# Two attention blocks on one core: later key blocks' scores from differences of keys, in pairs of tiles

## The chip, the cores and the metric

One core of one Trainium2 chip runs the kernel. The metric is device time in microseconds of one execution; the input arrays lie in device memory, laid out by the host, and the result is written back there. The granted clock of TensorE was full (1.00) in every stretch of the profile of the kernel before.

## The reference

Input x is 4 images of 64 channels with 32 x 32 positions, float32. Two layers follow each other, each for every image by itself:

```
h = group_norm(x, 32 groups) * gamma + beta
q, k, v = h Wq + bq, h Wk + bk, h Wv + bv         # 1024 positions, 64 channels
attn = softmax(q k^T / 8) v                       # 1024 x 1024 scores
x = x + attn Wo + bo
```

The two layers differ in their parameters and in the small constant under the root.

## The kernel before

A **unit** is one layer of one image; there are 8, and unit u+4 takes the result of unit u. An image lies in 128 partitions: the 64 channels of positions 0 to 511 in the upper half (rows 0 to 63), those of 512 to 1023 in the lower. So every product with 64 channels takes half the rows of TensorE's array, and two such products, one in each half of the rows, can go together.

Queries and keys are computed by `project` (L789) into `ps_scores[0]`. ScalarE (`high_front`, `high_back`, L380 to L389) writes them rounded to f32r, TensorE's fast number type, and VectorE (`low_front`, `low_back`, L570 to L582) what the rounding lost. `front` holds queries in its upper rows and keys in its lower rows, `back` the other way round, and `cross` gets the halves exchanged by four DMAs of 128 KB. The column halves are named HI and LO: the rounded part and the rest. The three buffers of each form a ring.

Softmax needs the greatest score of each query. `partial_max` (L808) computes rounded scores of 128 queries against 512 keys, twice, into the one buffer `ps_max`, 8 rounds per unit; after each, `part` (L584) on VectorE reduces 1024 columns. `join` brings the results together, `turn_max` (L829) transposes them, `stage_max` (L425) copies them, and `place_rows` (L229) writes them by DMA as a row `q_row`. The rounds for unit w+1 are spread over the loop of unit w, and the first two of unit w+2 follow in the same loop (`next_max(8)` and `next_max(9)`).

Scores come per tile of 128 keys against all 1024 queries, 8 tiles in a unit, in two alternating buffers `ps_scores` (in the last unit three). `scores_main` (L837) issues six half-array products of 512 columns: rounded by rounded, rounded keys by rest, rest by rounded queries. `scores_row` (L862) adds the negative maxima by two more products, `ones_r` by `q_row`. `exp` (L431) on ScalarE writes `probs[t]`; `values` (L874) on TensorE adds the tile's part of the result to `ps_attn`, and GpSimd (`add`, L306) sums the eight tiles, after `first_add` (L614) on VectorE. From the sum `denominators` (L904) makes column sums in 256 columns, two `reciprocal`s (L621) of 128 columns each invert them, eight DMAs spread them over the partitions as `rden`, and `finish` (L315) on GpSimd scales the result and adds x.

The order on every engine is written out by hand; each engine runs its list in order and stops at a wait on a semaphore. In the loop of TensorE (L1053) two or three steps of scores, maxima and values alternate; the projection for unit w+2 stands in the middle, after scores(w, 5).

Of the kernel before, what the change touches and what calls it, by code (L numbers as in the profile page):

```python
# [5 lines left out]
ALU = mybir.AluOpType  # L6
# [5 lines left out]
P = 128  # L12
# [18 lines left out]
def attention_pair(nc, x, layer_params, consts, out):  # L31
# [6 lines left out]


    B, _, HALF = x.shape  # L40
    N = 2 * HALF
    TILES = N // P
    UNITS = LAYERS * B
    LAST = UNITS - 1
    SCALE = float(C) ** -0.5
    JS = HALF // P
    POOL_ADDS = TILES - 2
    TAIL_ADDS = (4, 1)
    HEAD_MAX = [0, 1, 2, JS, JS + 1, JS + 2, 3, JS + 3]
    READY = 3 * P  # L50

    with ExitStack() as ctx:
# [13 lines left out]
        back_w = [sb(f"back_w{n}", [P, P]) for n in range(LAYERS)]  # L66
        back_bias = [sb(f"back_bias{n}", [P, 1]) for n in range(LAYERS)]
        const_sb = sb("const_sb", [P, 2 * P])
        ident = const_sb[:, 0:P]
        ones = sb("ones", [P, 2 * P])  # L70
        ones_r = sb("ones_r", [P, P], F32R)
        minus_half = sb("minus_half", [P, 1])
# [12 lines left out]
        front = [sb(f"front{b}", [P, N], F32R) for b in range(RING)]  # L85
        back = [sb(f"back{b}", [P, N], F32R) for b in range(RING)]
        cross = [sb(f"cross{b}", [P, N], F32R) for b in range(RING)]
        full_front = sb("full_front", [P, HALF])
        full_back = sb("full_back", [P, HALF])
        q_row = [sb(f"q_row{b}", [P, HALF], F32R) for b in range(2)]  # L90
# [3 lines left out]
        max_cols = sb("max_cols", [P, TILES * C])  # L94
# [5 lines left out]
        pick = sb("pick", [P, 4 * C])  # L100
        quarter_rden = sb("quarter_rden", [P, HALF // 2])
# [4 lines left out]
        ps_attn = psum("ps_attn", [P, HALF])  # L106
        ps_misc = psum("ps_misc", [P, HALF])
# [5 lines left out]
        ones_r_set = sem("ones_r_set")  # L113
        half_set = sem("half_set")
# [3 lines left out]
        cols_zero = sem("cols_zero")  # L118
        pick_zero = sem("pick_zero")
        pick_set = sem("pick_set")  # L120
        back_set = sem("back_set")
# [10 lines left out]
        front_hi = sem("front_hi")  # L132
        back_hi = sem("back_hi")
        front_full = sem("front_full")
        back_full = sem("back_full")
        front_lo = sem("front_lo")
        back_lo = sem("back_lo")
        first_back_hi = sem("first_back_hi")
        head_front_lo = sem("head_front_lo")
        head_back_lo = sem("head_back_lo")  # L140
# [9 lines left out]
        head_turned = sem("head_turned")  # L150
# [13 lines left out]
        quarter_done = sem("quarter_done")  # L164
# [11 lines left out]

        def halves():
            return (slice(0, HALF), slice(HALF, N))
# [13 lines left out]
        HI, LO = slice(0, HALF), slice(HALF, N)  # L192

        def back_hi_of(unit):
            return (back_hi, unit) if unit else (first_back_hi, 1)
# [7 lines left out]
        def scores_buffer(unit, t):  # L203
            return ps_scores[t % 2] if unit < LAST else (ps_scores[0], ps_scores[1], ps_max)[t % 3]
# [4 lines left out]
        def _(sp):  # L209
# [5 lines left out]
            def swap_hi(u):  # L215
                t = cross[u % RING]
                sp.wait_ge(front_hi, u + 1)
                sp.dma_start(t[0:C, HI].bitcast(F32), front[u % RING][C:P, HI].bitcast(F32)).then_inc(hi_swapped[u % RING], 16)
                sp.wait_ge(*back_hi_of(u))
                sp.dma_start(t[C:P, HI].bitcast(F32), back[u % RING][0:C, HI].bitcast(F32)).then_inc(hi_swapped[u % RING], 16)  # L220

            def swap_lo(u):
                t = cross[u % RING]
                sp.wait_ge(*low_count(front_lo, head_front_lo, u))
# [4 lines left out]
            def place_rows(u):  # L229
                sp.wait_ge(max_staged, u + 1)  # L230
                if u == 1:
                    sp.wait_ge(rows_zero, 1)
# [32 lines left out]
            for w in range(UNITS):  # L265
                if w:
                    spread_rden(w - 1)
                if w + 2 < UNITS:
                    swap_hi(w + 2)
                    swap_lo(w + 2)  # L270
# [915 lines left out]
```

## Time and profile before

| | |
|---|---|
| median of 3 runs | 185.75 us (185.75 to 185.83) |
| span of the profiled execution | 184.0 us (its total time is not on the page) |
| instructions | 3303 |
| TensorE busy | 174.6 us, 95% |
| VectorE busy | 138.3 us, 75% |
| GpSimd busy | 121.8 us, 66% |
| ScalarE busy | 100.4 us, 55% |

The span goes from the first to the last instruction. Engines are named PE (TensorE; PEld its weight loads), DVE (VectorE), ACT (ScalarE), POOL (GpSimd) and SP. Waiting is not busy time. The rows print f32r products as f32; the lines tell them apart. An f32 product appears as two instructions, its two passes.

### The profile page before, as it was taken

The page shows a single profiled execution, that of the slowest core. Times are in us where ns is not written, and L with a number is a line of the kernel's source. Part 1 is how long each engine was busy: PE and PEld are TensorE (multiplying, and loading weights), DVE is VectorE, ACT ScalarE, POOL GpSimd, SP SyncE. Part 2 cuts the span into 40 slices and gives each one's busy share as a digit, 9 for nine tenths or more (in the row PEclk, how much of TensorE's full clock was granted, in tenths as well). Part 3 has the DMA queues.
Part 4 walks back from the last instruction along what each step waited for, and adds up shares of the span by engine and source line. Part 5 has one row for each costly group of instructions (what it writes and reads, how often), then busy time and mean ns, then how long its engine had stood idle before and what let it go on. Part 6 is the DMA issues. An engine that isn't in the chain of part 4 may idle for free.

```text
span 184.0 us, 3303 instructions
## 1 busy us (share of the span) xinstructions
PE 174.6 (95%) x1223; PEld 93.5 (51%) x1223; DVE 138.3 (75%) x208; ACT 100.4 (55%) x137; POOL 121.8 (66%) x81
## 2 busy tenths in 40 slices
PE   7778899999999999999999999999999999999993
PEld 4435545555525644455535645555535555456661
DVE  2799987779887687859875787769875588386763
ACT  3479367606656376436666476527656554466500
POOL 5265017996799929996699949996799939705000
PEclk9999999999999999999999999999999999999999
DMA  5544100500016000420025000500025100110111
GB/s 154 189 100 98 34 2 0 114 4 2 0 34 142 2 0 14 102 60 0 0 54 122 0 4 20 136 18 0 5 59 115 61 0 21 37 61 7 50 57 57
DMA packets 7103, 8.89 MB, mean 48 GB/s; under 512 B 1656, under 2 KB 4144, under 8 KB 7088
## 3 DMA queue, kind: packets, MB, share of 16 engines
q1 hardware_dynamic: 6080, 7.84, 16.9%
q10 hardware_dynamic: 1008, 0.86, 1.6%
q8 instruction: 9, 0.15, 0.3%
q14 instruction: 6, 0.05, 0.1%
HBM read 1.58 MB, written 1.05 MB: 14 GB/s over the span
## 4 chain that ended last, share of the span: by engine, by line
PE 82%; DVE 13%; DMA 1%; issue 1%; POOL 0%; ACT 0%; DVEq 0%; POOLq 0%
PE ps_attn L887 27%; PE ps_max L817 9%; DVE part_max L588 8%; PE ps_scores L855 8%; PE ps_scores L871 7%; PE ps_scores L857 7%; PE ps_scores L859 7%; PE ps_scores L796 3%; PE ps_misc L804 2%; PE ps_attn L894 2%; PE ps_misc L900 2%; DMA xs<-x_dram 1%; PE ps_misc L894 1%; DVE quarter_rden L628 1%; PE ps_misc L831 1%
## 5 line engine op out<-in xcount | busy, mean ns | idle before, releaser
L313 POOL TENSOR_TENSOR prob_sum<-prob_sum,probs 128x1024 f32<-128x1024 f32 x41 | 97.5, 2377 | 29.0 <-ACT probs L441 16.8
L588 DVE TENSOR_REDUCE part_max<-ps_max 128x2 f32<-128x1024 f32 x60 | 73.4, 1224 | 26.3 <-PE ps_max L818 25.8
L441 ACT ACTIVATE probs<-ps_scores 128x1024 f32<-128x1024 f32 x62 | 61.0, 1025 | 46.1 <-PE ps_scores L872 45.4
L887 PE MATMUL ps_attn<-probs,vals 128*64 128x512 f32 x224 | 54.5, 605 | 0.0
L887 PEld LDWEIGHTS ps_attn<-probs,vals 128*64 128x64 f32 x224 | 13.5, 136 | 27.8 <-issue 19.2
L871 PE MATMUL ps_scores<-q_row,ones_r 64*128 64x512 f32 x62 | 24.5, 396 | 0.5 <-ACT q_row L423 0.5
L872 PE MATMUL ps_scores<-q_row,ones_r 64*128 64x512 f32 x62 | 24.6, 396 | 0.0
L817 PE MATMUL ps_max<-back,front 64*128 64x512 f32 x31 | 13.9, 449 | 2.3 <-DVE part_max L588 1.4
L817 PE MATMUL ps_max<-cross,front 64*128 64x512 f32 x29 | 14.6, 505 | 0.3 <-DVE part_max L588 0.3
L818 PE MATMUL ps_max<-cross,back 64*128 64x512 f32 x29 | 14.6, 505 | 0.0
L818 PE MATMUL ps_max<-front,back 64*128 64x512 f32 x31 | 14.0, 450 | 0.0
L628 DVE RECIPROCAL quarter_rden<-ps_misc 128x128 f32<-128x128 f32 x14 | 12.6, 930 | 1.1 <-PE ps_misc L900 1.1
L871 PEld LDWEIGHTS ps_scores<-q_row,ones_r 64*128 64x128 f32 x62 | 11.4, 184 | 3.2 <-issue 0.7
L856 PE MATMUL ps_scores<-back,cross 64*128 64x512 f32 x31 | 12.9, 418 | 0.0
L294 POOL TENSOR_TENSOR rstd<-var_eps,minus_half 128x1 f32<-128x1 f32 x8 | 4.4, 549 | 12.9 <-DVE var_eps L543 12.9
L855 PE MATMUL ps_scores<-front,back 64*128 64x512 f32 x31 | 12.9, 415 | 0.0
L855 PE MATMUL ps_scores<-front,cross 64*128 64x512 f32 x31 | 12.4, 399 | 0.0
L856 PE MATMUL ps_scores<-back,front 64*128 64x512 f32 x31 | 12.4, 399 | 0.0
L860 PE MATMUL ps_scores<-back,cross 64*128 64x512 f32 x31 | 12.1, 392 | 0.0
L859 PE MATMUL ps_scores<-front,back 64*128 64x512 f32 x31 | 12.1, 391 | 0.0
L860 PE MATMUL ps_scores<-back,front 64*128 64x512 f32 x31 | 12.1, 390 | 0.0
L859 PE MATMUL ps_scores<-front,cross 64*128 64x512 f32 x31 | 12.1, 390 | 0.0
(157 smaller groups left out, 365.7 us busy)
## 6 DMA issues: line engine op xcount, KB each, us to landing
cross<-front SPq DMA_DIRECT2D x16, 128.0 KB, 2.3
cross<-back SPq DMA_DIRECT2D x16, 128.0 KB, 2.3
rden<-quarter_rden SPq DMA_DIRECT2D x44, 32.0 KB, 1.8
xs<-x_dram SPq DMA_DIRECT2D x4, 256.0 KB, 4.6
out_dram<-xs SPq DMA_DIRECT2D x3, 256.0 KB, 2.0
rden<-quarter_rden ACTq DMA_DIRECT2D x12, 32.0 KB, 1.9
q_row<-max_rows SPq DMA_DIRECT2D x14, 2.0 KB
layer<-layers_dram SPq DMA_DIRECT2D x1, 194.5 KB, 2.7
```

The source lines that it names most:

```text
L313: pool.tensor_tensor(total[:, :], total[:, :], probs[t][:, :], ALU.add).then_inc(added, 1)
L441: act.activation(probs[t][:, :], scores_buffer(u, t)[:, :], ACT.Exp, scale=SCALE).then_inc(exp_done, 1)
L588: dve.tensor_reduce(part_max[u % 2][:, at:at + 2 * JS + 1:2 * JS], ps[:, :].rearrange("p (g n) -> p g n", g=2), AX.X, ALU.max, negate=True ...
L817: pe.matmul(ps[:, HI], f[top, tile], (x if crossed else g)[top, HI], start=True, stop=True)
L818: pe.matmul(ps[:, LO], g[low, tile], (x if crossed else f)[low, HI], start=True, stop=True).then_inc(max_mm, 1)
L855: pe.matmul(left, key_top[top, hi], front_u[top, HI], start=True, stop=False)
L856: pe.matmul(right, key_low[low, hi], back_u[low, HI], start=True, stop=False)
L859: pe.matmul(left, key_top[top, lo], front_u[top, HI], start=False, stop=False)
L860: pe.matmul(right, key_low[low, lo], back_u[low, HI], start=False, stop=False)
L871: pe.matmul(left, ones_r[top, :], row[top, :], start=False, stop=True)
L872: pe.matmul(right, ones_r[low, :], row[low, :], start=False, stop=True).then_inc(scores_mm, 1)
L887: mm = pe.matmul(ps_attn[half * C:(half + 1) * C, :], v, probs[t][:, cols], start=(t == 0), stop=(t == TILES - 1))
```

## The change

1. **Tiles in pairs.** Tile t now stands for key block `(t % 2, JS - 1 - t // 2)`: the two tiles of a pair are the same block in the two halves of the keys, and both score buffers fill together. The first pair's scores are computed in full. For pairs 1 to 3 the products with *differences* between neighbouring key blocks are added to the scores that still stand in the buffers. A pair waits for both exponentials of the pair before it, not for one of two tiles before.
2. **Row products once per unit.** As the negative maxima stay in the buffers, `add_rows` adds them once, after the first pair, by 4 products in place of 16. `q_row` is 1024 columns wide. In unit 0 `add_maxima` does it by 16 products of 128 columns against the identity; `turn_first` and `stage_first` go.
3. **Queries exchanged.** `q_hi`, `q_lo` hold queries in all 128 rows, `x_hi`, `x_lo` the same with the halves exchanged (four DMAs as before); the keys `k_hi`, `k_lo` are followed by their three differences, 384 columns. `project` makes four products of 64 x 64, and from unit 2 on writes `ps_max` instead of `ps_scores[0]`. ScalarE does high_queries, whole_keys, high_keys, high_differences; VectorE low_queries, key_differences, low_keys.
4. **Maxima.** No maximum of unit w+2 runs in the loop of unit w any more; project(w+2) is the last but one step of the loop.
5. **Denominators in 128 columns.** Eight products of 128 columns with a 0/1 pattern `parity` in place of four of 256, one reciprocal in place of two, eight DMAs of 64 x 128.
6. In the last unit the scores no longer use `ps_max` as a third buffer.

The core of the diff:

```diff
             def project(u):
-                p = layer[u // B]
+                p, ps = layer[u // B], ps_scores[0] if u < HEAD else ps_max
                 pe.wait_ge(h_ready, u + 1)
...
+                elif u >= HEAD:
+                    pe.wait_ge(max_done, TILES * u)
+                wq, wk = slice(WQ, WQ + C), slice(WK, WK + C)
+                pe.matmul(ps[TOP, HI], p[TOP, wq], h[TOP, :], start=True, stop=True)
+                pe.matmul(ps[LOW, HI], p[LOW, wq], h[LOW, :], start=True, stop=True)
+                pe.matmul(ps[LOW, LO], p[TOP, wk], h[TOP, :], start=True, stop=True)
+                pe.matmul(ps[TOP, LO], p[LOW, wk], h[LOW, :], start=True, stop=True).then_inc(proj_mm, 1)
...
             def partial_max(u, m, ps=ps_max):
...
+                if u:
+                    pe.wait_ge(max_done, TILES * u + m - (m == 0 and u == 1))
                 if m == 0:
-                    pe.wait_ge(front_hi, u + 1)
-                    pe.wait_ge(*back_hi_of(u))
+                    pe.wait_ge(q_hi_set, u + 1)
+                    pe.wait_ge(*k_hi_of(u))
+                    if u >= HEAD:
+                        pe.wait_ge(k_full_set, u + 1)
+                        pe.wait_ge(q_lo_set, u + 1 - HEAD)
...
+            def product(u, p, keys, at, in_place, exchanged, start, done):
+                block = slice(at, at + P)
+                top, low = ps_scores[1], ps_scores[0]
...
+            def pair_high(u, p):
+                b = u % RING
+                at = DIFF + p * P if p == 0 else HALF + (JS - 1 - p) * P
+                product(u, p, k_hi[b], at, q_hi[b], x_hi[b], p == 0, False)
+                product(u, p, k_hi[b], at, q_lo[b], x_lo[b], False, False)
+
+            def pair_low(u, p):
...
+                mm = product(u, p, k_lo[b], at, q_hi[b], x_hi[b], False, True)
...
+            def pair(u, p):
+                pe.wait_ge(exp_done, TILES * u + 2 * p)
+                pair_high(u, p)
+                pair_low(u, p)
```

`product` issues four half-array products of 512 columns: keys of the upper rows into the two banks of `ps_scores[1]`, those of the lower rows into `ps_scores[0]`. The loop of TensorE for units 1 to 6 is now, in this order (w the unit, the maxima those of w+1):

```
first_pair(w)  max 0  pair_low(w, 0)  add_rows(w)  max 1  values(w-1, 6) values(w-1, 7)  max 2
pair(w, 1)  max 3  denominators(w-1)  values(w, 0) values(w, 1)  max 4  pair(w, 2)  max 5
values(w, 2) values(w, 3)  max 6  pair(w, 3)  max 7  values(w, 4) values(w, 5)  turn_max(w+1)
project(w+2)  project_v(w+2)
```

ScalarE's loop ends with exp(w, 6), exp(w, 7), stage_max(w+1), high_queries(w+2), whole_keys, high_keys, copy_v, high_differences. VectorE's is part 0, part 1, low_keys(w+1), own_stats(w+2), part 2, share_stats, join_stats, first_add(w), part 3, affine, part 4, reciprocal(w-1), parts 5 to 7, join(w+1), low_queries(w+2), key_differences.

TensorE at the end of a unit, before, from the transposition of unit 3's maxima on:

```order
L831 MATMUL ps_misc<-const_sb,neg_max 8x128 [waits max_joined,quarter_done]
L817 MATMUL ps_max<-back,front 128x512 [waits back_hi,front_hi,max_done]
L818 MATMUL ps_max<-front,back 128x512
L855 MATMUL ps_scores<-front,back 128x512 [waits exp_done,back_lo,front_lo]
L856 MATMUL ps_scores<-back,cross 128x512
L857 MATMUL ps_scores<-front,back 128x512
```

and in the changed kernel, from the same transposition:

```order
L809 MATMUL ps_both<-const_sb,neg_max 8x128 [waits rden_done,max_joined]
L774 MATMUL ps_max<-h,layer 64x512 [waits max_done,h_ready]
L775 MATMUL ps_max<-h,layer 64x512
L776 MATMUL ps_max<-h,layer 64x512
L777 MATMUL ps_max<-h,layer 64x512
L783 MATMUL ps_both<-wvo,h 64x128 [waits max_staged]
L783 MATMUL ps_both<-wvo,h 64x128 x7
```

Before, a maximum of the next unit and scores follow the transposition; now the projection into ps_max and that of the values do.

TensorE in the changed kernel a little later, from the last products of the projection of values to the first maximum of the next unit:

```order
L783 MATMUL ps_both<-wvo,h 64x128 x7
L814 MATMUL ps_scores<-q_hi,k_hi 128x512 [waits exp_done,k_lo_set,lo_swapped0]
L816 MATMUL ps_scores<-q_hi,k_hi 128x512
L818 MATMUL ps_scores<-x_hi,k_hi 128x512
L820 MATMUL ps_scores<-x_hi,k_hi 128x512
L814 MATMUL ps_scores<-q_lo,k_hi 128x512
L816 MATMUL ps_scores<-q_lo,k_hi 128x512
L818 MATMUL ps_scores<-x_lo,k_hi 128x512
L820 MATMUL ps_scores<-x_lo,k_hi 128x512
L802 MATMUL ps_max<-k_hi,q_hi 128x512 [waits k_full_set,k_hi_set,q_lo_set,q_hi_set,max_done]
L803 MATMUL ps_max<-k_hi,q_hi 128x512
```

The first maximum waits for five semaphores of ScalarE and VectorE; 8 score products stand ahead of it and 8 products behind it before the next maximum.

VectorE at the same boundary, before (neg_max is join's result, the lines after it make front's and back's rest):

```order
L611 TENSOR_REDUCE neg_max<-part_max 128x8 [waits max_turned,max_done]
L572 SCALAR_TENSOR_TENSOR front<-ps_scores,layer,front 128x512 [waits front_hi]
L579 SCALAR_TENSOR_TENSOR back<-ps_scores,back_bias,back 128x512 [waits back_hi]
L588 TENSOR_REDUCE part_max<-ps_max 128x2 [waits max_mm] x2
L522 BN_STATS stats<-xs 128x6 [waits final_done]
L588 TENSOR_REDUCE part_max<-ps_max 128x2 [waits max_mm]
```

and in the changed kernel:

```order
L623 TENSOR_REDUCE neg_max<-part_max 128x8 [waits max_turned,max_done]
L590 SCALAR_TENSOR_TENSOR q_lo<-ps_max,bias_q,q_hi 128x512 [waits q_hi_set]
L597 TENSOR_TENSOR k_full<-k_full 128x384 [waits k_full_set]
L609 TENSOR_REDUCE part_max<-ps_max 128x2 [waits max_mm] x2
L602 TENSOR_TENSOR k_lo<-k_full,k_hi 128x512 [waits d_hi_set,k_hi_set]
L541 BN_STATS stats<-xs 128x6 [waits final_done]
L609 TENSOR_REDUCE part_max<-ps_max 128x2 [waits max_mm]
```

low_front and low_back, which both stood ahead of the next rounds, became low_queries and key_differences there, and low_keys after the second round; `BN_STATS` moved behind it.

## Rows read from the trace of the kernel before

**Rows 1.** The page, busy us of each engine, share of the span, instructions.
```profile
PE 174.6 (95%) x1223; PEld 93.5 (51%) x1223; DVE 138.3 (75%) x208; ACT 100.4 (55%) x137; POOL 121.8 (66%) x81
```

**Rows 2.** Busy us in a steady stretch, by engine: stretch, busy (instructions).
```profile
96.50:117.00 20.50, 20.50 (x143) 10.68 (x141) 15.93 (x25) 11.85 (x15) 17.25 (x10) 1.00 0.18 41
```

**Rows 3.** The page, chain that ended last, share of the span by engine.
```profile
PE 82%; DVE 13%; DMA 1%; issue 1%; POOL 0%; ACT 0%; DVEq 0%; POOLq 0%
```

**Rows 4.** The page, groups of instructions: shapes, count, busy us, mean ns, idle before.
```profile
L588 DVE TENSOR_REDUCE part_max<-ps_max 128x2 f32<-128x1024 f32 x60 | 73.4, 1224 | 26.3 <-PE ps_max L818 25.8
L628 DVE RECIPROCAL quarter_rden<-ps_misc 128x128 f32<-128x128 f32 x14 | 12.6, 930 | 1.1 <-PE ps_misc L900 1.1
```

**Rows 5.** Waits: who waited for whom, us in total, times, longest.
```profile
PEld ps_max L817 <- DVE part_max L588: 13.9, 24, 1.2
```

**Rows 6.** Timeline of TensorE, one unit: start us, us, engine, line, operation, tiles, shapes.
```profile
96.95 0.50 PE L817 MATMUL ps_max<-back,front 64*128 64x512 f32 x1
97.29 0.39 PE L855 MATMUL ps_scores<-front,back 64*128 64x512 f32 x1
97.52 0.39 PE L857 MATMUL ps_scores<-front,back 64*128 64x512 f32 x1
...
104.73 1.94 PE L887 MATMUL ps_attn<-probs,vals 128*64 128x512 f32 x8
106.60 0.50 PE L817 MATMUL ps_max<-cross,front 64*128 64x512 f32 x1
...
117.23 0.27 PE L831 MATMUL ps_misc<-const_sb,neg_max 128*8 128x128 f32 x1
117.43 0.50 PE L817 MATMUL ps_max<-back,front 64*128 64x512 f32 x1
```

**Rows 7.** Timeline of TensorE: a maximum that waited, and the denominators.
```profile
23.37 0.49 PE L817 MATMUL ps_max<-back,front 64*128 64x512 f32 x1 [0.39 <-DVE part_max L588]
...
109.31 0.64 PE L900 MATMUL ps_misc<-prob_sum,ones 128*32 128x256 f32 x8
```

**Rows 8.** Timeline of VectorE, same unit as in rows 6.
```profile
97.50 1.23 DVE L588 TENSOR_REDUCE part_max<-ps_max 128x2 f32<-128x1024 f32 x1 [0.62 <-PE ps_max L818]
...
103.91 0.16 DVE L527 STREAM_SHUFFLE stats<-stats 128x6 f32<-128x6 f32 x1
...
105.04 1.21 DVE L588 TENSOR_REDUCE part_max<-ps_max 128x2 f32<-128x1024 f32 x1
106.17 1.21 DVE L618 TENSOR_TENSOR prob_sum<-probs 128x1024 f32<-128x1024 f32 x1
```

**Rows 9.** Timeline of ScalarE: exponentials of units 0, 6 and 7.
```profile
21.85 2.19 ACT L441 ACTIVATE probs<-ps_scores 128x1024 f32<-128x1024 f32 x2 [0.71 <-PE ps_scores L872]
...
144.63 1.95 ACT L441 ACTIVATE probs<-ps_scores 128x1024 f32<-128x1024 f32 x2 [3.31 <-PE ps_scores L872]
...
162.25 1.95 ACT L441 ACTIVATE probs<-ps_scores 128x1024 f32<-128x1024 f32 x2 [1.96 <-PE ps_scores L872]
...
172.54 1.96 ACT L441 ACTIVATE probs<-ps_scores 128x1024 f32<-128x1024 f32 x2 [1.99 <-PE ps_scores L872]
```

**Rows 10.** Groups of instructions by line and shape: busy us, mean ns, idle before.
```profile
L408 ACT ACTIVATE vals<-ps_misc 128x512 f32<-128x512 f32 x8 | 4.7, 593 | 0.0
...
L572 DVE SCALAR_TENSOR_TENSOR front<-ps_scores,layer,front 128x512 fp32r<-128x512 f32 x6 | 4.5, 745 | 0.9 <-ACT front L383 0.9
```

**Rows 11.** Timeline of TensorE and ScalarE around the projection of a later unit.
```profile
113.21 0.69 PE L796 MATMUL ps_scores<-h,layer 64*128 64x512 f32 x1
113.75 0.59 PE L796 MATMUL ps_scores<-h,layer 64*128 64x512 f32 x1
...
114.45 0.69 ACT L383 ACTIVATE front<-ps_scores,layer 128x512 fp32r<-128x512 f32 x1
```

**Rows 12.** Timeline of ScalarE and TensorE: a staged row and its use.
```profile
38.25 0.27 ACT L429 ACTIVATE max_rows<-ps_misc 8x128 fp32r<-8x128 f32 x1 [1.28 <-PE ps_misc L831]
...
41.00 0.47 PE L871 MATMUL ps_scores<-q_row,ones_r 64*128 64x512 f32 x1
```

More of the change, by code:

```diff
@@ L750, in _ @@
                 part(w + 1, 4)
+                reciprocal(w - 1)
                 part(w + 1, 5)
[L752 to L755 removed]
+                part(w + 1, 6)
+                part(w + 1, 7)
+                join(w + 1)
                 if prep:
[L757 to L764 removed]
+                    low_queries(w + 2)
+                    key_differences(w + 2)
             finish_tail(LAST - 2)
@@ L862, in scores_row @@
[L862 to L872 removed]
+                if u > 1:
+                    pe.wait_ge(rden_done, u - 1)
@@ new lines, in pair, with add_rows @@
+            def pair(u, p):
+                pe.wait_ge(exp_done, TILES * u + 2 * p)
+                pair_high(u, p)
+                pair_low(u, p)
+            def add_rows(u):
+                row = q_row[u % 2]
+                pe.wait_ge(row_in[u % 2], last_row(u))
+                for side in (HI, LO):
+                    pe.matmul(ps_scores[1][:, side], ones_r[TOP, :], row[TOP, side], start=False, stop=True,
+                              skip_group_check=True)
+                    mm = pe.matmul(ps_scores[0][:, side], ones_r[LOW, :], row[LOW, side], start=False, stop=True,
+                                   skip_group_check=True)
+                mm.then_inc(scores_mm, 1)
@@ L874, in values, with add_maxima @@
+            def add_maxima(blocks):
+                for j in blocks:
+                    for n in range(2):
+                        t = n * JS + j
+                        for ps in ps_scores:
+                            mm = pe.matmul(ps[:, t * P:(t + 1) * P], neg_first[:, t:t + 1].broadcast_to([P, P]),
+                                           ident_r[:, :], start=False, stop=True, skip_group_check=True)
+                return mm
             def values(u, t):
@@ L975, in _ @@
             head_max(7)
+            first_pair(0)
+            pair_low(0, 0)
+            partial_max(1, 0)
+            pe.wait_ge(ident_set, 1)
             pe.wait_ge(head_joined, 1)
[L977 to L984 removed]
@@ L1066, in _ @@
+            for w in range(1, LAST):
+                prep = w + 2 < UNITS
+                first_pair(w)
+                partial_max(w + 1, 0)
+                pair_low(w, 0)
+                add_rows(w)
+                partial_max(w + 1, 1)
                 values(w - 1, 6)
                 values(w - 1, 7)
-                next_max(4)
-                scores(w, 2)
-                scores(w, 3)
-                next_max(5)
+                partial_max(w + 1, 2)
+                pair(w, 1)
+                partial_max(w + 1, 3)
```

762 lines of the change are left out of this document (317 added, 445 removed).

## The prediction, made before the changed kernel had run

> **What bounds the kernel now.** I read the shares first: TensorE is busy 174.6 of 184.0 us, VectorE 138.3, GpSimd 121.8, ScalarE 100.4 [rows 1]. In a steady stretch of 20.5 us TensorE is busy all of it, VectorE 15.93, ScalarE 11.85, GpSimd 17.25 [rows 2], and the chain that ended last is 82% TensorE, 13% VectorE [rows 3]. So TensorE's own work sets the pace, and a second engine is near: VectorE's 60 reductions of 1024 columns take 73.4 us [rows 4], and TensorE's maxima wait for them 24 times, 13.9 us in all [rows 5]; that row is of the weight loads, which run ahead, so most of this is hidden now. One unit takes 117.43 - 96.95 = 20.48 us from its first maximum to the next one's [rows 6].
>
> Prices on TensorE [rows 6]: two half-array products together step by 0.23 us (97.29 to 97.52), 0.34 for the first after another shape (96.95 to 97.29). Two tiles of values, with the changes of shape, take 1.87 (104.73 to 106.60). A maximum that has waited runs about 0.50 before its result is usable [rows 7]. The reduction is then 1.23, and a handover costs about 0.05 (the maximum's end at 97.45 to 97.50 [rows 6, 8]); I take the same for the way back. **A round of one maximum is therefore 0.50 + 0.05 + 1.23 + 0.05 = 1.83 us**, and no order of TensorE's work gets below it, since one buffer holds the maxima in both kernels.
>
> **The change, part by part.**
> *Row products.* Per tile two row-adding products go, 16 per unit, and 4 return (add_rows): 8 pair steps less 2, so 6 x 0.23 = 1.4 us less TensorE work per unit. The score products are as many as before, 12 for two tiles. A little comes back: a change of shape for the projection, and eight sums in place of four in the denominators, at about 0.1 each (the first step's 0.34 less 0.23). TensorE's own work falls by 1.2 us, to 19.3.
>
> *Pairs.* Both score buffers now fill together, and a pair waits for the exponentials of both tiles before it. Two exponentials take 1.95 us [rows 9]; between two pairs TensorE has a maximum, two tiles of values and another maximum, 0.34 + 1.87 + 0.34 = 2.5 us, which covers them. In the middle of a unit I charge nothing; in unit 7, where no maxima are left, the cover is values alone.
>
> *The maxima's loop.* Here the gain goes. The projection of unit w+2 now writes ps_max, so it must follow the last maximum of unit w+1, and the first maximum of w+2 must follow the copies out of that buffer. Before, the projection sat in a score buffer in mid unit, and two maxima ran ahead across the boundary. Now the eight rounds and the projection form one closed chain per unit. Laid out, with m0 to m7 for the maxima:
> - m0 to m1: product 0.39, then 0.05 + 1.23 + 0.05 = 1.72. TensorE has only pair_low and the rows to do there (4 x 0.23).
> - m1 to m4: VectorE does, start to start, 0.55 until the part begins, part 1.13, low_keys 0.66, bn_stats 0.66 (both as the 512-column form of 745 ns less 0.08, by which one instruction runs into the next), part 1.13, the small statistics 1.13, first_add 1.14, the last part 1.21 + 0.05 [rows 8, 10]: 7.7. TensorE's work there (values, pair, denominators 0.6, values, three maxima) is 6.9.
> - m4 to m5 and m6 to m7: pair plus maximum is 6 x 0.23 + 0.34 = 1.72, under a round, so 1.83 each. m5 to m6: 0.34 + 0.09 + 1.87 = 2.3, TensorE's.
> - m7 to the next m0: 0.45 to leave the maximum, 1.87 values, 0.25 turn; projection 1.1 (113.21 to 114.34), handover 0.11 (to 114.45); high_queries and whole_keys 0.69 each less 0.1 overlap [rows 11], high_keys 0.6 (a copy of 512 columns, 593 ns [rows 10]), two handovers 0.1: 5.8. TensorE's project_v and first_pair, 1.0 each, are hidden under these copies.
>
> Sum 1.72 + 7.7 + 1.83 + 2.3 + 1.83 + 5.8 = **21.2 us per unit against 20.48, +0.7**. Five loops have this steady form: **+3.5 us**. What TensorE saved, and more, is spent waiting for max_done and k_hi_set.
>
> *VectorE's parts.* One reciprocal of 128 columns goes (0.93 us [rows 4]); low_front and low_back (0.745 each [rows 10]) become low_queries, key_differences and low_keys (0.745, 0.57 for 384 of the 512 columns, 0.745). The total falls by 0.4 us, but the reciprocal stood where TensorE had other work, while low_keys stands between two rounds: in the chain nothing is gained.
>
> *ScalarE and the queues.* ScalarE gains two copies per unit (1.1 us); with 8.6 idle of 20.5 [rows 2] only those before m0 count, and they are in the loop. The exchanges of queries are four transfers of 128 KB as those of the keys and queries were, needed later than m0; rden stays eight issues of 32 KB, now in 64 pieces each for 32, ahead of the rows and exchanges on SP as before. In the loop a staged row is used more than 3 us later and takes 2.5 (below): nothing charged. GpSimd's 17.25 [rows 2] fit in 21.2. Were its cover gone, at a loop under 17.3, it would bound.
>
> *Head.* turn_first, its copies into q_row and unit 0's 16 row products go; 16 products of 128 columns over the whole array come, a form in f32r that the trace lacks. The lower bound is 0.06 each (a quarter of the 0.23 of 512 columns), the upper 0.27, an f32 product of 128 columns [rows 6]; I take 0.13, nearer the same number type. With the longer chain on GpSimd the first exponential, now at 21.85 [rows 9], comes **0.3 us later**, bounds -0.7 and +3.
>
> *Boundary into unit 7.* No projection covers the last rows any more. After m7: 0.45 + 1.87 values, turn 0.27, handover 0.1, copy 0.27; from a staged row to its use 2.5 (38.52 to 41.00 [rows 12]); two row steps 0.8: the exponential is 6.2 us after m7. From m0 to m7 there are no statistics left, so TensorE's 6.9 stands for the 7.7: 14.6. Unit 6's exponential comes 1.5 after m0. That makes 19.3 from exponential to exponential; now it is 162.25 - 144.63 = 17.6 [rows 9]. **+1.7 us**, most of it TensorE waiting for row_in.
>
> *Tail.* Now the last exponential ends at 174.5, 12.3 after unit 7's first [rows 9]. In pairs it is four times two exponentials 2.0 and a pair with its handovers 1.6, without the first pair, plus some 1.7 for the values' wait for rden_done: 14.5. Behind it one reciprocal less, -0.9. **+1.3 us.**
>
> Total 3.5 + 0.3 + 1.7 + 1.3 = 6.8: a span of 190.8 us for 184.0. The page gives no total time of its execution, only the span; the median run of 185.75 is 1.75 above it, and I keep that. **Forecast 192.5 us.**
>
> **Where a page speaks against the change.** The projection is now four quarter-array products, the first two of them in one bank of ps_max and from different halves of the rows. The trace has no such form; the nearest are its two half-array products into two banks, 0.53 and 0.59 a pass [rows 11], and four column strips side by side in the denominators, 0.64 for all [rows 7]. By these rows I take all four as concurrent, 1.1 us.
> The Trainium skill, "TensorEngine Tiling (Array Packing)", Restrictions and Gotchas, says that different row tiles cannot access the same PSUM bank simultaneously. No run here shows it for such products. By it the first two would go one after another, and the sum would be rival 1's.
>
> **Rivals.**
> 1. *The quarter-array products don't run together.* Each further slot costs two passes of 0.54 between starts less the first step's 0.1 (113.21 to 113.75 [rows 11]), 0.9 us, in six later projections and about once in the head: 6 us for two slots, 12 for three. The time is 198.5, at worst 204. For: a bank and the rows are shared. Against: column strips run together in values and denominators.
> 2. *TensorE stays the bound (faster).* If low_keys and the statistics fall into VectorE's idle time (4.6 of 20.5 [rows 2]) and the copies before m0 run under TensorE's work, a unit costs TensorE's 19.3, and the change gives 1.2 x 7 = 8.4, less 3 for boundary and tail: 180 us. It decides at a loop below 20.48, that is if the stretch m1 to m4 takes under 7.0. Against: each instruction in the loop has a row, and the order on VectorE is fixed.
> 3. *Half of the loop is slack.* The loop is about today's 20.5 and only head, boundary and tail count, or part of them: 185 to 189.
> 4. *It does not do what it says*, the accumulated differences needing waits of their own: a pair already waits for both exponentials, so nothing more is needed; no chance of its own.
>
> **How the numbers follow.** Forecast 0.56 (189 to 195.5), rival 1 0.16, rival 2 0.12, rival 3 0.16. Of rival 3 about 0.02 is faster and 0.04 within 0.2%, 0.4 us, about what a measurement of this kernel can tell from no change. Faster 0.14, same 0.04, slower 0.82. The range leaves out most of rival 2 and the upper part of rival 1: 186.5 to 199.
>
> **What would show it.** Right: a steady unit of about 21.2 us; ps_max waiting for part_max in most rounds, and for k_hi once per unit; TensorE's share down to about 90%; a wait of over 1 us for q_row before unit 7; the first exponential near 22.2; the four projection products within 1.1 us, which also decides against rival 1. Wrong: a steady unit at or under 20.5 with TensorE still full; a first exponential after 25; pairs that wait for exponentials in mid unit, for which I charge nothing.

## The result, and the profile after

The changed kernel takes **199.67 us** (199.42 to 200.76, 4 runs) where before takes 185.78: a ratio of **1.0745**, 95% interval 1.0718 to 1.0772. Executions of one kernel scatter; the ratios here leave out those more than 1.5% above its fastest, the medians keep them. The sign of the forecast was right and its mechanism is there. Its size was not: +13.9 us for the forecast +6.7, and just outside the range (199.0).

The page of the profile after, first the shares, then the chain by engine; then the wait that answers to [rows 5] and a steady stretch that answers to [rows 2]:

```profile
PE 172.4 (87%) x1227; PEld 85.5 (43%) x1227; DVE 144.1 (73%) x206; ACT 107.0 (54%) x149; POOL 131.3 (66%) x82
...
PE 53%; DVE 31%; issue 9%; DMA 2%; ACT 2%; SPq 0%; POOL 0%; DVEq 0%; ACTq 0%; POOLq 0%
```
```profile
PEld ps_max L802 <- DVE part_max L609: 41.0, 49, 1.9
```
```profile
109.50:132.10 22.60, 20.25 (x141) 9.58 (x141) 17.36 (x24) 12.94 (x18) 18.58 (x10) 1.00 0.16 36
```

TensorE is no longer full. It waits for the maxima's reductions 49 times, 41.0 us, for 24 times and 13.9 before, and VectorE's share of the chain has gone from 13% to 31%. That row is of the weight loads, which run ahead; TensorE's products themselves stood idle for the same releaser 21 times, 13.5 us, for 5 times and 1.7 before. VectorE itself is 1.4 us busier per unit than in [rows 2], although the forecast had its list 0.4 us shorter.

How long a unit takes is read from the first exponential of each, on ScalarE's timeline after:

```profile
22.92 1.94 ACT L462 ACTIVATE probs<-ps_scores 128x1024 f32<-128x1024 f32 x2 [1.80 <-PE ps_scores L869]
...
42.71 1.94 ACT L462 ACTIVATE probs<-ps_scores 128x1024 f32<-128x1024 f32 x2 [0.76 <-PE ps_scores L860]
...
63.89 1.94 ACT L462 ACTIVATE probs<-ps_scores 128x1024 f32<-128x1024 f32 x2 [0.56 <-PE ps_scores L860]
...
86.52 1.94 ACT L462 ACTIVATE probs<-ps_scores 128x1024 f32<-128x1024 f32 x2 [0.58 <-PE ps_scores L860]
...
154.43 1.94 ACT L462 ACTIVATE probs<-ps_scores 128x1024 f32<-128x1024 f32 x2 [0.59 <-PE ps_scores L860]
174.87 1.94 ACT L462 ACTIVATE probs<-ps_scores 128x1024 f32<-128x1024 f32 x2 [3.35 <-PE ps_scores L860]
```

From unit 1 to unit 2 it is 63.89 - 42.71 = **21.18 us, the forecast 21.2**. The next four are 22.63 each (86.52 - 63.89; 154.43 - 63.89 is four of them). Two loops with the same list of instructions differ by 1.45 us, so the question is what differs between them. They differ in one stretch: from maximum 1 to maximum 4 (starts on TensorE's timeline) it is 50.62 - 43.07 = 7.55 us in the first and 118.50 - 109.50 = 9.00 in a later one, for 7.7 forecast.

```profile
43.07 0.50 PE L802 MATMUL ps_max<-k_hi,q_hi 64*128 64x512 f32 x1 [0.40 <-DVE part_max L609]
...
50.62 0.50 PE L802 MATMUL ps_max<-k_hi,x_hi 64*128 64x512 f32 x1 [0.46 <-DVE part_max L609]
...
109.50 0.49 PE L802 MATMUL ps_max<-k_hi,q_hi 64*128 64x512 f32 x1 [0.39 <-DVE part_max L609]
...
118.50 0.49 PE L802 MATMUL ps_max<-k_hi,x_hi 64*128 64x512 f32 x1 [0.47 <-DVE part_max L609]
```

VectorE in the slow loop:

```profile
110.04 1.23 DVE L609 TENSOR_REDUCE part_max<-ps_max 128x2 f32<-128x1024 f32 x1 [0.59 <-PE ps_max L803]
111.18 2.13 DVE L602 TENSOR_TENSOR k_lo<-k_full,k_hi 128x512 fp32r<-128x512 f32 x1
113.24 0.68 DVE L541 BATCH_NORM_STATS2 stats<-xs 128x6 f32<-128x512 f32 x1
...
116.10 1.22 DVE L630 TENSOR_TENSOR prob_sum<-probs 128x1024 f32<-128x1024 f32 x1
```

and in the loop from unit 1 to 2:

```profile
44.76 0.68 DVE L602 TENSOR_TENSOR k_lo<-k_full,k_hi 128x512 fp32r<-128x512 f32 x1
```

The same instruction, same shapes, takes 0.68 us once and 2.13 later. The view of that line shows that the once is the exception (duration in ns, min/median/max, then the first and last start):

```profile
L602 DVE TENSOR_TENSOR k_lo<-k_full,k_hi x6: 681/2126/2152, 44.8 to 156.5; 128x512 fp32r<-128x512 f32 x6
```

GpSimd's timeline around both, first at the short one, then at the long one:

```profile
28.12 15.18 POOL L330 TENSOR_TENSOR prob_sum<-prob_sum,probs 128x1024 f32<-128x1024 f32 x6 [1.90 <-DVE prob_sum L630]
48.26 1.58 POOL L305 TENSOR_TENSOR rstd<-var_eps,minus_half 128x1 f32<-128x1 f32 x1 [4.96 <-DVE var_eps L561]
...
107.55 5.21 POOL L330 TENSOR_TENSOR prob_sum<-prob_sum,probs 128x1024 f32<-128x1024 f32 x2
116.14 1.58 POOL L305 TENSOR_TENSOR rstd<-var_eps,minus_half 128x1 f32<-128x1 f32 x1 [3.37 <-DVE var_eps L561]
```

At 44.76 GpSimd is idle (43.30 to 48.26). At 111.18 it is in its second add, which ends at 112.76, and low_keys ends 0.55 later: as if it had started only then. The same the other way round: one element per partition, rstd, takes 1.58 us when VectorE's first_add (116.10 to 117.32) runs, and 0.55 otherwise. That is **theory A**: a VectorE operation with two operands in SBUF and a GpSimd operation exclude each other, so that the later one waits until the other instruction has ended, and low_keys stands in the one place where its delay goes straight into the closed loop of maxima. Rivals: low_keys is slow by itself, in its types or its neighbours (**B**); TensorE's own work sets the interval anyhow (**C**).

### The profile page after: what moved, and what is told of

The parts are those of the page before. It is cut to its first block, busy times and chain, and to the rows that moved or that the text cites. A ratio compares the mean times of both kernels' runs of the same rounds, so it can differ in the third digit from the quotient of the medians.

```text
span 197.6 us, 3324 instructions
## 1 busy us (share of the span) xinstructions
PE 172.4 (87%) x1227; PEld 85.5 (43%) x1227; DVE 144.1 (73%) x206; ACT 107.0 (54%) x149; POOL 131.3 (66%) x82
## 3 DMA queue, kind: packets, MB, share of 16 engines
HBM read 1.58 MB, written 1.05 MB: 13 GB/s over the span
## 4 chain that ended last, share of the span: by engine, by line
PE 53%; DVE 31%; issue 9%; DMA 2%; ACT 2%; SPq 0%; POOL 0%; DVEq 0%; ACTq 0%; POOLq 0%
PE ps_both L886 14%; DVE part_max L609 14%; PE ps_max L802 10%; PE ps_scores L814 8%; PE ps_scores L818 6%; DVE k_lo L602 5%; PE ps_both L783 4%; DVE prob_sum L630 3%; PE ps_max L774 3%; DVE stats L541 2%; PE ps_scores L820 2%; ACT probs L462 2%; DMA xs<-x_dram 1%; DVE moments L557 1%; PE ps_both L893 1%
## 5 line engine op out<-in xcount | busy, mean ns | idle before, releaser
L886 PE MATMUL ps_both<-probs,vals 128*64 128x512 f32 x224 | 54.2, 605 | 0.0
L802 PE MATMUL ps_max<-k_hi,q_hi 64*128 64x512 f32 x31 | 15.0, 485 | 12.7 <-DVE part_max L609 11.0
L886 PEld LDWEIGHTS ps_both<-probs,vals 128*64 128x64 f32 x224 | 13.6, 136 | 22.7 <-issue 20.4
L802 PEld LDWEIGHTS ps_max<-k_hi,q_hi 64*128 64x128 f32 x31 | 5.7, 183 | 26.8 <-DVE part_max L609 21.6
L802 PE MATMUL ps_max<-k_hi,x_hi 64*128 64x512 f32 x29 | 14.4, 496 | 2.5 <-DVE part_max L609 2.5
L803 PE MATMUL ps_max<-k_hi,q_hi 64*128 64x512 f32 x31 | 15.3, 493 | 0.0
L803 PE MATMUL ps_max<-k_hi,x_hi 64*128 64x512 f32 x29 | 14.4, 495 | 0.0
L814 PE MATMUL ps_scores<-q_hi,k_hi 64*128 64x512 f32 x32 | 13.7, 428 | 0.3 <-ACT probs L462 0.3
L816 PE MATMUL ps_scores<-q_hi,k_hi 64*128 64x512 f32 x32 | 13.7, 428 | 0.0
L814 PE MATMUL ps_scores<-q_lo,k_hi 64*128 64x512 f32 x32 | 12.5, 392 | 0.0
L818 PE MATMUL ps_scores<-x_hi,k_hi 64*128 64x512 f32 x32 | 12.5, 391 | 0.0
L820 PE MATMUL ps_scores<-x_hi,k_hi 64*128 64x512 f32 x32 | 12.5, 391 | 0.0
L816 PE MATMUL ps_scores<-q_lo,k_hi 64*128 64x512 f32 x32 | 12.5, 391 | 0.0
L818 PE MATMUL ps_scores<-x_lo,k_hi 64*128 64x512 f32 x32 | 12.5, 390 | 0.0
L820 PE MATMUL ps_scores<-x_hi,k_lo 64*128 64x512 f32 x32 | 12.5, 389 | 0.0
```

The source lines that it names most:

```text
L802: pe.matmul(ps[:, top], q[TOP, tile], k[TOP, 0:HALF], start=True, stop=True)
L803: pe.matmul(ps[:, low], q[LOW, tile], k[LOW, 0:HALF], start=True, stop=True).then_inc(max_mm, 1)
L814: pe.matmul(top[:, HI], keys[TOP, block], in_place[TOP, :], start=start, stop=done, skip_group_check=True)
L816: pe.matmul(low[:, LO], keys[LOW, block], in_place[LOW, :], start=start, stop=done, skip_group_check=True)
L818: pe.matmul(top[:, LO], keys[TOP, block], exchanged[TOP, :], start=start, stop=done, skip_group_check=True)
L820: return pe.matmul(low[:, HI], keys[LOW, block], exchanged[LOW, :], start=start, stop=done, skip_group_check=True)
```

## The experiments

Twelve runs. Ratios are to the kernel before on the same chip (its medians there 185.78 to 186.52), and the runs were made on several chips, so the ratios are to be compared rather than the medians. "low_keys" is the median duration of that operation in units 2 to 7; "interval" is from one unit's first exponential to the next one's in units 2 to 6.

| run | ratio (95%) | median us | low_keys us | interval us |
|---|---|---|---|---|
| changed kernel | 1.0745 (1.0718 to 1.0772) | 199.67 | 2.13 | 22.63 |
| e10 the same again | 1.0739 (1.0711 to 1.0767) | 199.82 | 2.14 | 22.64 |
| e1 low_keys later | 1.0529 (1.0498 to 1.0561) | 196.74 | 0.68 | 21.74 |
| e2 low_keys on GpSimd | 1.0366 (1.0338 to 1.0394) | 193.44 | 1.29, GpSimd | 21.17 |
| e3 low products twice | 1.0715 (1.0680 to 1.0749) | 199.62 | 2.14 | 22.64 |
| e4 whole keys on VectorE | 1.0783 (1.0710 to 1.0855) | 201.66 | 0.68 to 2.44 | 21.16 to 25.13 |
| e5 work dealt out | 1.0240 (1.0193 to 1.0288) | 190.95 | 0.68 | 20.76 |
| e6 short adds | 1.0332 (1.0285 to 1.0378) | 192.92 | 0.68 | 21.17 |
| e7 values before rows | 1.0291 (1.0204 to 1.0379) | 193.91 | 0.68 | 20.76 |
| e8 early denominators | 1.0205 (1.0179 to 1.0231) | 189.78 | 0.68 | 20.76 |
| e9 high keys on VectorE | 1.0177 (1.0116 to 1.0238) | 189.79 | 0.68 | 20.45 |
| e11 clearing later | 1.0696 (1.0637 to 1.0756) | 198.78 | 2.15 | 22.65 |
| e12 all reorderings | 1.0071 (1.0040 to 1.0102) | 187.79 | 0.68 | 20.44 |

**e10: the base line again.**

> The changed kernel once more, unaltered, beside the others on their chip, as the base line for the differences: 199.7 us where before has 185.8 us, a ratio of 1.07 to 1.077.

As expected.

**e1: low_keys moved into GpSimd's idle time.**

```diff
                 part(w + 1, 1)
-                low_keys(w + 1)
                 if prep:
                     own_stats(w + 2)
                 part(w + 1, 2)
+                low_keys(w + 1)
```

> VectorE's subtraction of key blocks (low_keys) moved from behind part 1 to behind part 2 of each unit, where the profile of the changed kernel shows GpSimd idle (112.76 to 116.14 us); nothing else is altered. Theory A (a VectorE operation with two operands in SBUF and a GpSimd operation exclude each other): low_keys falls from 2.13 us to 0.68 us, the interval between first exponentials of units 4 to 7 from 22.63 to about 21.2 us, the whole from 199.7 to 192 to 194 us. Rival B (low_keys is slow by its own types and strides): it stays at 2.1 us, intervals 22.6, whole 199 to 200 us. Rival C (TensorE or another engine sets the interval): low_keys gets short but the whole moves by less than 1 us.

VectorE's and GpSimd's timelines of e1:

```profile
111.20 0.69 DVE L541 BATCH_NORM_STATS2 stats<-xs 128x6 f32<-128x512 f32 x1
112.35 1.23 DVE L609 TENSOR_REDUCE part_max<-ps_max 128x2 f32<-128x1024 f32 x1 [0.47 <-PE ps_max L803]
113.50 0.68 DVE L602 TENSOR_TENSOR k_lo<-k_full,k_hi 128x512 fp32r<-128x512 f32 x1
```
```profile
107.57 5.22 POOL L330 TENSOR_TENSOR prob_sum<-prob_sum,probs 128x1024 f32<-128x1024 f32 x2
```

0.68 us, so B in its plain form falls. The interval lost 0.9 us and not 1.45: VectorE now waits 0.47 us for maximum 2, which stands behind TensorE's 1.87 us of values. In its old place low_keys, were it short, would have filled that wait. bn_stats, with one operand in SBUF, ran beside the adds and took its usual 0.69. The loop from unit 1 to 2, where low_keys had been short already, got longer by the move, 21.73 for 21.18 (65.67 - 43.94 in e1): by itself the new place costs 0.55 us, since that wait is no longer filled. The whole, 196.74, is above the 192 to 194 expected, mostly for this reason.

**e6: low_keys in its old place, GpSimd idle.** The sums of tiles 6 and 7 of units 1 to 5 are taken over 8 columns in place of 1024, so most of them is left out.

```diff
-                pool.tensor_tensor(total[:, :], total[:, :], probs[t][:, :], ALU.add).then_inc(added, 1)
+                cols = slice(0, 8 if 0 < u < LAST - 1 and t > 5 else N)
+                pool.tensor_tensor(total[:, cols], total[:, cols], probs[t][:, cols], ALU.add).then_inc(added, 1)
```

> VectorE's order as in the changed kernel, but GpSimd's adds for key tiles 6 and 7 of units 1 to 5 take 8 columns instead of 1024, so that those sums leave most of two tiles out; GpSimd is then idle while low_keys runs in its old place. Theory A (exclusion): low_keys 0.68 us where it was 2.13, interval about 21.7 us as with low_keys moved, time over before 1.05 to 1.055. Rival B2 (low_keys is slow in its old place for another reason, such as fresh operands or its neighbours on VectorE): it stays at 2.1 us, interval 22.6, 1.074.

VectorE and GpSimd in e6:

```profile
109.18 0.68 DVE L603 TENSOR_TENSOR k_lo<-k_full,k_hi 128x512 fp32r<-128x512 f32 x1
...
112.64 1.21 DVE L631 TENSOR_TENSOR prob_sum<-probs 128x1024 f32<-128x1024 f32 x1
```
```profile
105.57 0.87 POOL L331 TENSOR_TENSOR prob_sum<-prob_sum,probs 128x8 f32<-128x8 f32 x2
112.68 1.58 POOL L305 TENSOR_TENSOR rstd<-var_eps,minus_half 128x1 f32<-128x1 f32 x1 [6.24 <-DVE var_eps L562]
```

Nothing on VectorE was touched, and low_keys falls to 0.68. **B falls in every form; A is shown.** The interval is 21.17 in all five loops, that of the one undisturbed loop of the changed kernel and what the forecast said; my own expectation of 21.7 had overlooked the wait just told. rstd still takes 1.58, since VectorE's first_add is there first. The whole, 192.92 us, is the forecast 192.5 but for 0.4, in part by luck: the head came 0.8 and unit 6 0.3 above the forecast, the first loop 0.75 and the tail 0.3 below it (the account is further down).

**e3: more work for TensorE.** `pair_low(w, 0)` stands twice.

> The four products with the low halves of the first key pair are issued twice in units 1 to 6, which counts the low correction of that pair double; TensorE gets about 0.46 to 0.5 us of columns more per unit, in the stretch where it otherwise waits 0.55 us for part 0. Theory A (loop of maxima through VectorE sets the interval): interval unchanged at 22.6 us, whole 199.5 to 200.3 us. Rival C (TensorE bound): 0.46 x 6 = 2.8 us more, 202.5 us.

22.64, as in e10, and a ratio of 1.0715 for 1.0739 (e10 ran on another chip), the intervals overlapping: 24 more products cost nothing. **C falls for this kernel**: TensorE is off the path between maxima 0 and 1, where they were added, and what it saves or adds there does not move the interval.

**e2: low_keys on GpSimd.** `low_keys(w + 1)` heads GpSimd's step for unit w, ahead of `root(w + 2)`, and leaves VectorE's list.

> low_keys for units 2 to 7 issued by GpSimd, in front of its reciprocal root, instead of by VectorE. Theory A (mutual exclusion, and the loop of maxima through VectorE sets the interval): the operation takes 1.3 us on GpSimd in its idle time, VectorE loses 2.13 us per unit, interval 20.5 to 20.7 us, whole 189 to 191 us. Rival B (low_keys slow by itself, loop closed through VectorE): the same 189 to 191 us, so it is told apart by the run with low_keys moved. Rival C (TensorE sets the interval): less than 1 us of gain, 199 us.

GpSimd in e2:

```profile
105.79 5.22 POOL L330 TENSOR_TENSOR prob_sum<-prob_sum,probs 128x1024 f32<-128x1024 f32 x2
110.96 1.29 POOL L320 TENSOR_TENSOR k_lo<-k_full,k_hi 128x512 fp32r<-128x512 f32 x1
112.91 1.58 POOL L305 TENSOR_TENSOR rstd<-var_eps,minus_half 128x1 f32<-128x1 f32 x1 [0.66 <-DVE var_eps L563]
```

The operation costs what was expected, in idle time; the interval is 21.17 and not 20.6, by the same 0.48 us wait for maximum 2. Counting only VectorE's list, as I did, overstates a gain where TensorE is next in line.

**e4: whole keys on VectorE.** `whole_keys` of units 2 to 7 stands ahead of `low_queries` on VectorE.

> The whole keys of units 2 to 7 written by VectorE (bias added, from PSUM) while ScalarE writes the high queries; ScalarE then writes the high keys directly. The chain from the turn of the maxima to the next unit's first maxima loses one of three ScalarE steps of 0.58 to 0.63 us and gets at most 0.1 us of hand-over back. Theory A: last to first maxima falls from 5.89 to about 5.4 us, whole 199.7 - 6 x 0.5 = 196.5 us (195.8 to 197.3). Rival C (TensorE bound): no change, 199 to 200 us. Rival D (VectorE's low queries come later by the new step, 0.7 us): last to first maxima stays at 5.9 us, no change.

Slower. VectorE and GpSimd of e4, and two stretches (their columns as in [rows 2]):

```profile
84.42 0.75 DVE L589 SCALAR_TENSOR_TENSOR q_lo<-ps_max,bias_q,q_hi 128x512 fp32r<-128x512 f32 x1
85.09 2.73 DVE L606 TENSOR_TENSOR k_full<-k_full 128x384 f32<-128x384 f32 x1
87.75 1.21 DVE L618 TENSOR_REDUCE part_max<-ps_max 128x2 f32<-128x1024 f32 x1
```
```profile
83.77 1.29 POOL L339 TENSOR_TENSOR xs<-attn,xs 128x512 f32<-128x512 f32 x1
85.03 5.02 POOL L330 TENSOR_TENSOR prob_sum<-prob_sum,probs 128x1024 f32<-128x1024 f32 x2
```
```profile
70.00:72.00 2.00, 2.00 (x22) 0.76 (x22) 1.97 (x5) 0.00 (x0) 1.45 (x1) 0.67 0.00 0
72.00:74.00 2.00, 2.00 (x6) 0.24 (x2) 1.15 (x3) 0.81 (x1) 2.00 (x2) 0.50 0.00 0
```

The first maximum does come 0.3 us earlier behind the last (79.98 to 85.56, 5.58 for 5.86 to 5.89). But low_keys, which starts earlier in its add, now takes up to 2.44 us (2.41 at 65.31), and behind one such low_keys TensorE waited 1.7 us for part 2, from 67.8 to 69.5; then its granted clock was 0.67 and 0.50 in these stretches, the level of 1.2 GHz. In the next boundary key_differences falls just behind the start of an add and takes 2.73 us where 0.55 to 1.11 were seen, and part 0 waits behind it. The interval with all three, the long low_keys, the fallen clock and the long key_differences, is 25.13; one with a low_keys of 2.44 alone is 22.65. q_lo, one operand in PSUM, keeps its 0.75 beside GpSimd. What made the clock fall is not shown: in the same profile it stayed at 1.00 after waits of 2.13 us (to 89.02) and 1.73 us (to 115.81). None of my theories had this outcome.

**e5: VectorE's work dealt out.** Behind part 0 own_stats and share_stats, behind part 1 join_stats, behind part 2 low_keys and first_add, behind part 3 affine.

> The extra VectorE work of a unit dealt out over the gaps of the loop of maxima: own_stats and share_stats behind part 0, join_stats behind part 1, low_keys and first_add behind part 2, affine behind part 3. From the run with low_keys moved: each gap hides 0.6 us under TensorE's next maxima, and 0.5 us more behind parts 0 and 4, 1.1 us more behind part 2, where TensorE has values or denominators to do. Theory A (loop through VectorE, and the exclusion with GpSimd): nothing sticks out any more, interval 20.7 us (from 21.7 with low_keys moved alone), time over before 1.025 to 1.032, about 191 to 192.5 us where before has 186.5. Rival C (only the exclusion mattered, the order does not): as with low_keys moved, 21.7 us and 1.053.

As expected, 20.76. On GpSimd rstd no longer meets first_add:

```profile
103.29 5.21 POOL L330 TENSOR_TENSOR prob_sum<-prob_sum,probs 128x1024 f32<-128x1024 f32 x2
108.47 0.54 POOL L305 TENSOR_TENSOR rstd<-var_eps,minus_half 128x1 f32<-128x1 f32 x1
```

**e7 and e8: the last unit.** e7 is e5 with `values(LAST - 1, 6)` and `(LAST - 1, 7)` ahead of `add_rows(LAST)`; e8 also has `denominators(LAST - 1)` ahead of `pair(LAST, 1)`, and on VectorE `reciprocal(LAST - 1)` ahead of `first_add(LAST)`.

> As the run with VectorE's work dealt out, and in the last unit the two value products of the unit before stand ahead of the product with the row of maxima, which waits for its DMA. Theory: the wait of 1.36 us (1.8 us for the weight load) before that row is filled by 1.87 us of values; the time falls by 1.1 to 1.5 us against the run with the work dealt out alone, 1.018 to 1.025 over before. Rival: the last unit is bound by its exponentials or by the late sums on VectorE, which start later by 0.5 us; then the time stays or grows by 0.5 us.

> As the run with values ahead of the last rows, and the denominators of the unit before the last stand ahead of the last unit's pair 1, their reciprocal ahead of first_add on VectorE. In the profile of the run before, TensorE waits 2.03 us for the first two exponentials of the last unit and 1.08 us for the reciprocal. Theory: both waits are filled, 0.6 us by the denominators and 1.08 us because the reciprocal runs under the exponentials: 1.5 to 1.9 us less from the last unit's first exponential to the end (from 22.8 to about 21.1 us), span about 187.6 us. Rival: the late sums on VectorE, which start 1 us later behind the reciprocal, set the end; then 0 to 0.7 us.

e7 was a miss; its runs scatter, so its profile, at full clock, is compared with that of e5: it took 42.78 us from unit 6's first exponential to the end for 42.34 in e5. Its timeline of TensorE shows why:

```profile
168.52 0.50 PE L814 MATMUL ps_scores<-q_hi,k_hi 64*128 64x512 f32 x1 [2.03 <-ACT probs L462]
```

The wait for the row was filled and a wait of 2.03 us for the first two exponentials took its place, since the values had covered that. e8 fills it: 21.20 us from the last unit's first exponential to the end for 22.77 in e7.

**e9: high keys on VectorE** straight from PSUM, ahead of `low_queries`; ScalarE's `whole_keys` follow.

> As the run with the early denominators, and VectorE writes the high keys of units 2 to 7 from PSUM beside ScalarE's high queries, ScalarE writes the whole keys behind them. The first maxima then wait for two steps (1.35 us) and not three (1.9 us) behind the projection; TensorE has at most 0.3 us of idle time there (103.16 + 0.23 to 103.68 us). Theory: interval 20.75 to about 20.45 us, 1.5 to 1.9 us in all, if key_differences stays short (0.83 us in the run with the work dealt out). Rival: key_differences meets GpSimd's adds, takes 2 us or more and delays part 0 as in the run with whole keys on VectorE; interval above 21 us.

Theory and rival both came in: 20.45 in four loops, with key_differences at 0.65; in the two intervals before them 21.05 and 22.06, where key_differences met an add (2.78 us, at 40.73) and the stretch 47 to 49 us then had a granted clock of 0.50. In the whole, 1.0177 is not told apart from the 1.0205 of e8: the intervals overlap.

**e11: the start.** In the changed kernel the clearing of `q_row`, twice as wide as before, runs beside VectorE's half of the first h. VectorE and GpSimd after:

```profile
6.34 1.47 DVE L579 TENSOR_SCALAR h<-xs,gain,shift 128x256 f32<-128x256 f32 x1
```
```profile
5.82 1.84 POOL L347 MEMSET q_row<- 128x1024 f32 x2
```

```diff
-            for n in range(2):
-                pool.memset(q_row[n][:, :].bitcast(F32), 0.0).then_inc(rows_zero, 1)
             root(1)
...
             root(2)
+            for n in range(2):
+                pool.memset(q_row[n][:, :].bitcast(F32), 0.0).then_inc(rows_zero, 1)
```

> The changed kernel with GpSimd's clearing of the two row buffers (1.84 us at 5.82 us) moved behind its third root; nothing else. In the changed kernel's profile VectorE's half of the first h takes 1.47 us (6.34 to 7.81 us) where before it took 0.41 us, and GpSimd clears until 7.66 us. Theory A, extended (this one-input VectorE operation from SBUF to SBUF and a GpSimd operation exclude each other too): h 0.41 us, first projection at about 7.0 us for 7.96, the first exponential at 21.9 to 22.1 us for 22.92 and 23.21, the whole 0.8 to 1.1 us shorter than the changed kernel, a ratio of 1.068 to 1.07. Rival: h is slow for another reason (its operands arrive late, the first instruction of its form): nothing changes, 1.074.

```profile
6.57 0.41 DVE L579 TENSOR_SCALAR h<-xs,gain,shift 128x256 f32<-128x256 f32 x1
```

In e11 (the row above) h takes 0.41, and the first exponential comes at 22.09. The median is 1.0 us under that of e10, on another chip, and the ratios' intervals overlap, so the row is the evidence, not the time. It shows that this form, one tensor read from SBUF and written to SBUF, is held too, and by an operation that only writes. In the profiled execution, the slowest of the four, unit 0's interval was 21.33 us for 19.79 and took back the 0.8 won: the granted clock was 0.50 from 26 to 28 us, and key_differences met an add (2.57 us at 40.39).

**e12: all of it.**

> All reorderings together: VectorE's work dealt out, values ahead of the last rows, early denominators, high keys on VectorE, and the clearing behind the third root. From the profiles: first exponential 22.0, then 19.8, 20.75 (22.1 if key_differences of unit 3 meets GpSimd's adds again as in the run before), 20.45 four times, 20.0, and 21.2 to the end: a span of 185.6 to 187 us, 187.4 to 188.8 us in all, 1.007 to 1.015 over before. Rival: below 186, faster than before, if the earlier head also takes the collision out of unit 1; by the sum it does not get there.

187.79 us, 1.0071 (1.0040 to 1.0102): about 12 of the 13.9 us are back by order, and by one copy moved from ScalarE to VectorE, with every product of the change as it was. The 12 executions scatter from 186.4 to 192.4, the three slowest with a granted clock of 0.971 or 0.972, the others with 0.986 to 1.00. No version beat the kernel before.

## Why the prediction was wrong

- **The step that failed** is the price of low_keys in the stretch m1 to m4: "low_keys 0.66 ... as the 512-column form of 745 ns". That form, low_front, reads one operand from PSUM [rows 10]; low_keys reads both from SBUF. Start to start it took 113.24 - 111.18 = **2.06 us**, and the stretch 9.00 for 7.7. What failed is the overlap: the sum put the meeting with GpSimd's add at nothing. Alone low_keys took 45.36 - 44.76 = 0.60, so the 0.66 was right where GpSimd was idle. In the loop of the kernel before only first_add was a wide operation with two operands in SBUF, the adds wait for it, and nothing showed the exclusion: rstd took 0.54 to 0.56 us in all its eight uses, GpSimd's 41 adds 2.35 to 2.40. I priced by type and columns and did not ask where the operands lie.
- The Trainium skill, "SBUF — State Buffer", section "Who interferes with whom", has the rule: a VectorE instruction with two SBUF inputs contends with a GpSimd instruction that reads SBUF, but not with one that only writes it. It calls the port pair that the two share an exclusive lock. The traces agree (0.68 to 2.13, and 0.55 to 1.58 the other way). It was a page that spoke against this change, and I had not weighed it. The sentence on two inputs does not cover e11, where the VectorE operation reads one tensor and GpSimd only writes.
- Everything else in the loop held: 21.18 measured in the undisturbed loop, 21.17 in e6, forecast 21.2. By stretches, in e6: m0 to m1 1.82 for 1.72, m1 to m4 7.55 for 7.7, m4 to m5 and m6 to m7 1.82 for 1.83, m5 to m6 2.30 for 2.3, m7 to m0 5.86 for 5.8. In m1 to m4 the sum has VectorE alone, though; e1 and e2 show TensorE's values next in line before maximum 2 (0.47 and 0.48 us of wait).
- **The account.** Forecast span 190.8, measured 197.6, 6.8 more. The head: 22.92 for 22.15, +0.8, and e11 shows it to be the clearing beside h (22.09 with the clearing later). Unit 0's interval +0.1. Units 1 to 6: 154.43 - 42.71 = 111.7 for 106.6, +5.1: four loops with +1.45, less 0.7 since the first of the five was slower than the others already before. Unit 6: 20.44 for 19.3, +1.1, of which 0.85 are low_keys again (19.59 in e6). The tail: 22.73 for 23.05, -0.3. The wait for the row of maxima before unit 7, forecast at over 1 us, was 1.36.
- **Rival 1** fell. The four quarter-array products of a projection start together, and the two passes take 105.32 - 104.30 = 1.02 us to the next product, for 1.1 in the sum. (Its own price for a further slot was a little low: 2 x 0.54 less 0.1 is 0.98, not 0.9.) TensorE after:

```profile
104.30 0.64 PE L774 MATMUL ps_max<-h,layer 64*64 64x512 f32 x1
104.31 0.64 PE L775 MATMUL ps_max<-h,layer 64*64 64x512 f32 x1
104.31 0.64 PE L776 MATMUL ps_max<-h,layer 64*64 64x512 f32 x1
104.32 0.64 PE L777 MATMUL ps_max<-h,layer 64*64 64x512 f32 x1
```

  The first two come from different halves of the rows and write one bank, in different partitions. So the measurement goes against the sentence of the Trainium skill, "TensorEngine Tiling (Array Packing)", Restrictions and Gotchas, as I had read it: neither waited for the other.
- **Rival 2** fell for the changed kernel (e3). Its 19.3 us of TensorE's own work was too low as well: in e5, where VectorE hides everything it can, the interval is 20.76 with 0.7 us of waits (0.40 for part 0, and 0.29 before the first maximum, which could start at 103.16 + 0.23 and starts at 103.68), so about 20.1. I have not taken the other 0.8 apart. **Rival 3** fell: no half of the loop was slack (21.17 in e6, with low_keys at its full speed, for 20.5).
- The pairs' waits for exponentials in mid unit, charged at nothing, were nothing. The 16 products of `add_maxima` took 2.00 us, 0.125 each, for 0.13.
- The range ended at 199.0, the result at 199.67: I had bounded the new forms of TensorE from both sides, but the new VectorE form by one row only.

## What to carry to other kernels

Price a VectorE instruction by where its operands lie, not only by columns and type: when the copy it reads moves from PSUM to SBUF, look at what GpSimd does at that moment. An instruction that exists once per loop can go to GpSimd in its idle time (e2), or on VectorE to a moment when GpSimd is idle and the other engine has work (e5). In a place that closes a loop beside a busy GpSimd, put only a form seen to run there unchanged: here those that read PSUM, bn_stats and the reductions. And in a loop of two engines, what a gap can hide depends on who is next in line: e5's steady loop is 0.98 us shorter than e1's (20.76 for 21.74) by the order on VectorE alone.

## What I had not expected of the hardware

- The exclusion works both ways, and the later instruction ends only after the other one has: VectorE's 0.68 became 2.13, GpSimd's 0.55 became 1.58, key_differences went up to 2.78 us (0.55 at its shortest).
- A one-operand VectorE operation from SBUF to SBUF of 256 columns was held from 0.41 to 1.47 us by GpSimd's clearing of a buffer, while bn_stats and reductions of the same engine ran beside GpSimd unchanged.
- A wait of 1.7 us of TensorE in the middle of full work was followed by stretches at half the granted clock (e4, 0.50 at 72 to 74 us), and waits of 1.7 and 2.1 us in the same profile were not. So a delay on VectorE may cost twice, but no run here shows when.
